# Scores of local attention per 32 queries, turned P through a raster of 512-byte blocks, q and k turned together

## The chip, the cores and the metric

The kernel runs on one NeuronCore of one Trainium2 chip, as one program. The metric is the device time of one execution in microseconds (us). Engine names are those of the profile: PE is TensorE's matmuls and PEld its weight loads, DVE is VectorE, ACT is ScalarE, POOL is GpSimd, SP is SyncE, which here issues nearly all DMAs.

## The reference, cut to what matters

The whole is a recurrent attention layer over 2 sequences of 4096 tokens with 256 channels, followed by two layers of windowed attention with a gated MLP. The change is inside the windowed attention, in each of those two layers:

```python
WINDOW, HEADS, DIM_HEAD = 128, 8, 64
def local_attention(q, k, v):               # q, k are normalised and rotated before
    bq = q.reshape(b, h, w, WINDOW, d) * QK_SCALE
    bk = look_around(k.reshape(b, h, w, WINDOW, d))   # window before + own: 256 keys
    bv = look_around(v.reshape(b, h, w, WINDOW, d))
    sim = einsum('bhwid,bhwjd->bhwij', bq, bk)
    mask = (i < j) | (i > j + WINDOW) | (j == -1)
    attn = softmax(where(mask, -max, sim))
    return einsum('bhwij,bhwjd->bhwid', attn, bv)
```

The mask leaves each query its own key and the 128 before it. A group of 32 neighbouring queries therefore needs at most 160 of the 256 keys of its two windows.

## The kernel before, in words

The program runs stages one after the other (setup, mix, scan, gate, local). The local stage does both layers. It works in units of one window: 128 tokens of one of the two sequences ("streams", `s`), 64 units (`u`, 32 for each layer) per stream, `w` is the unit's parity. The order of work of every engine is written out by hand in a function `half(s, u, w, l)`, of which there are 128. A half runs the attention scores and softmax of unit `u` of stream `s`, and beside them the rest (values, output projection, mean and variance, MLP) of the other stream's unit, called `o, um` in the code; it also projects the next unit of `s`. Engines wait for each other by semaphores alone.

Heads go in four pairs (`hp` 0 to 3). In a half these steps matter here:

- PE: `values(o, 0)`, `values(o, 1)`, `scores(s, 0)`, `scores(s, 1)`, in the second layer `turn_out`, then `values(o, 2)`, `values(o, 3)`, `scores(s, 2)`, `scores(s, 3)`, `project_out`, the three projections (L2473) with `mean` and `variance` between them, `hidden` (L2551, three groups), `out` (L2559). `scores` makes for each head of the pair one matmul, 64 partitions deep, with 128 queries as the stationary operand and 256 keys as the moving one. The two heads of a pair lie on partitions 0 to 63 and 64 to 127 and write two PSUM banks: B and C for even pairs, A of this stream and A of the other for odd ones. `scores(s, 3)` may start when `row_max(s, 1)` has emptied the A banks.
- DVE: `row_max` adds the mask to the scores in PSUM, writes them to `l_prob` in SBUF and takes the maximum in the same pass (L2186), then multiplies the pair's two maxima by a scale (`l_nb`, L2193). Later `inverse_sums` (L2173), the joining of the residual (`attended`, L2219), `deviate` (L2228), and `turn_p` (L2202), which transposes P within blocks of 32 by 32. `turn_q` and `turn_k` do the same for q and k.
- ACT: eight exponentials with row sums (L2367), one for each head, after `head_out` (L2376) has copied the other stream's values out of PSUM.
- POOL: the rotation of k (L2017 to L2022), `normalise` (P times the inverse row sums, L2033), `l_hn` (L2051), which `hidden` waits for, and more.
- SP: the blocks of 32 by 32 are put in their places by a way through DRAM: `write_p` (L1924) stores the turned P of two head pairs, one DMA of 512 KB, and `read_p` (L1932) reads it in four DMAs of 128 KB, one for each 32 partitions. `write_q`/`read_q` and `write_k`/`read_k` do that for q and k. In a half P goes in two groups `g` (pairs 0, 1 and pairs 2, 3); `values(2)` of the next half waits for the second.

The turned keys lie in two slots, `kT[s]`, of which unit `u` writes slot `w`; scores read both, and the mask (`mask[s][w]`, L2186) puts the slots in order. The mask for `w` = 0 is made anew in every second half (`remask`, L2213).

Of the kernel before, what the change touches and what calls it, by code (L numbers as in the profile page):

```python
# [21 lines left out]
ALU = mybir.AluOpType  # L22
# [3 lines left out]
P = 128  # L26
NB = 2
# [1718 lines left out]
def local_stage(nc, persist, a, T):  # L1746
# [7 lines left out]
    BL = P // 32  # L1754
    rows, const, ident = (persist[k] for k in ("rows", "const", "ident"))
    wqkv, wo, w1, w2, b1c, lngb, qks = (persist[k] for k in ("wqkv", "wo", "w1", "w2", "b1c", "lngb", "qks"))
    G = ((0, 1), (2, 3), (4, 5))
    with ExitStack() as ctx:
# [3 lines left out]
        wm = one("wm", [P, 2 * P])  # L1762
        mean_w, pause, least = one("mean_w", [P, P]), one("pause", [P, NB]), one("least", [P, 1])
        x1s, dsqs = two("x1s", [P, P]), two("dsqs", [P, P])
        mask = [two(f"mask{s}_", [P, 2, P]) for s in range(NB)]
# [5 lines left out]
        qT, kT = two("qT", [P, P, NHP]), two("kT", [P, 2, BL, NHP, 32])  # L1771
        V, prob = two("V", [P, 2, HEADS, DH]), two("prob", [P, HEADS, 2 * P])
        pb, pT = two("pb", [P, 2, BL, NHP, 2, 32]), two("pT", [P, 2, BL, NHP, 2, 32])
# [7 lines left out]
        sems = {n: ctx.enter_context(nc.semaphore(f"l_{n}")) for n in ("wm", "set", "prep", "zero", "free", "wqkv", "wo", "w1", "w2", "wiped0", "wiped1")}  # L1781
        R = signals(nc, ctx, "tab", 1, "lr")
        S = signals(nc, ctx, "q_ps k_ps v_ps qsq ksq v_sb ss_q ss_k clamped ln_n rn rq8 kn qm qr k12 kr q_turned k_turned "
                    "q_out:16 k_out:16 qT:64 kT:64 mask0 wo_ps carry x1 x1_sum mean_ps dev dsq dsq_sum var_ps ln_v rstd hn w2_ps hout "
# [61 lines left out]
        def scored(s, hp, x):  # L1846
            return ((bank[s][1], bank[s][2]), (bank[s][0], bank[1 - s][0]))[hp % 2][x][:, 0:2 * P]
# [4 lines left out]
        with nc.Block() as block:  # L1852
            @block.sync
            def _(sp):
# [30 lines left out]
                def write_q(s, u):  # L1885
# [3 lines left out]
                    sp.wait_ge(S["qT"][s].sem, S["qT"][s].after(u, 1))  # L1889
                    sp.sem_inc(sems["free"], 1)  # L1890
                    sp.dma_start(a["qz"][s], q1[s][:].rearrange("p h d -> p (h d)")).then_inc(S["q_out"][s].sem, 16)

                def read_q(s, u):
                    sp.wait_ge(S["q_out"][s].sem, S["q_out"][s].after(u))
                    sp.sem_inc(sems["free"], 1)
                    sp.wait_ge(Q["sc"][s].sem, Q["sc"][s].after(u * NHP - 1))
                    sp.sem_inc(sems["free"], 1)
                    for j in range(BL):
                        sp.dma_start(qT[s][32 * j:32 * j + 32].rearrange("p (i t) h -> p i (t h)", i=BL),
                                     a["qz"][s].rearrange("(i c) (j n) -> j c i n", i=BL, j=BL)[j]).then_inc(S["qT"][s].sem, 16)  # L1900

                def write_k(s, u):
                    sp.wait_ge(S["k_turned"][s].sem, S["k_turned"][s].after(u))
                    sp.sem_inc(sems["free"], 1)
                    sp.wait_ge(S["kT"][s].sem, S["kT"][s].after(u, 1))
                    sp.sem_inc(sems["free"], 1)
                    sp.dma_start(a["kz"][s], k1[s][:].rearrange("p h d -> p (h d)")).then_inc(S["k_out"][s].sem, 16)

                def read_k(s, u, w):
                    sp.wait_ge(S["k_out"][s].sem, S["k_out"][s].after(u))  # L1910
                    sp.sem_inc(sems["free"], 1)
                    sp.wait_ge(Q["sc"][s].sem, Q["sc"][s].after(u * NHP - 1))
                    sp.sem_inc(sems["free"], 1)
                    for j in range(BL):
                        sp.dma_start(kT[s][32 * j:32 * j + 32, w].rearrange("p i h t -> p i (h t)"),
                                     a["kz"][s].rearrange("(i c) (j n) -> j c i n", i=BL, j=BL)[j]).then_inc(S["kT"][s].sem, 16)
# [850 lines left out]
```

## Time and profile before

| what | us |
|---|---|
| median of three runs | 4972.72 (4967.94 to 4975.3) |
| the profiled execution | 4966.22 |
| its span | 4964.4 |
| local stage within it | from about 2257 to the end |

The profile covers one execution. Its span is 1.8 us shorter than that execution's own time, and that time is 6.5 us under the median. Busy time is the time in which an engine had an instruction running; matmuls are pipelined, so that a row's length holds some latency and rows overlap. Starts are us from the span's start. `[0.23 <-issue]` at the end of a row is how long its engine had been idle before it and what ended that.

### The profile page before, as it was taken

The page shows a single profiled execution, that of the slowest core. Times are in us where ns is not written, and L with a number is a line of the kernel's source. Part 1 is how long each engine was busy: PE and PEld are TensorE (multiplying, and loading weights), DVE is VectorE, ACT ScalarE, POOL GpSimd, SP SyncE. Part 2 cuts the span into 40 slices and gives each one's busy share as a digit, 9 for nine tenths or more (in the row PEclk, how much of TensorE's full clock was granted, in tenths as well). Part 3 has the DMA queues.
Part 4 walks back from the last instruction along what each step waited for, and adds up shares of the span by engine and source line. Part 5 has one row for each costly group of instructions (what it writes and reads, how often), then busy time and mean ns, then how long its engine had stood idle before and what let it go on. Part 6 is the DMA issues. An engine that isn't in the chain of part 4 may idle for free. (4 is left out here: it accounts for less than half of the span.)

```text
span 4964.4 us, 269505 instructions
## 1 busy us (share of the span) xinstructions
PE 4507.8 (91%) x107928; PEld 3817.4 (77%) x107928; DVE 3564.7 (72%) x10345; ACT 2979.7 (60%) x8486; POOL 2441.6 (49%) x3196
## 2 busy tenths in 40 slices
PE   7898898678888888666999999999999999999998
PEld 6888888678888888654777777777777777777777
DVE  4666666568878887475777777777777777777775
ACT  5777777534444444354666666666666666666665
POOL 1222222267777777203555555555555555555554
PEclk8999999789999999788999999999999999999999
DMA  2343343467777777694555666555565555555554
GB/s 87 87 96 93 93 98 89 114 143 165 165 165 163 167 164 161 175 299 126 170 170 168 173 174 171 172 171 171 180 196 175 173 173 172 171 171 173 173 175 131
DMA packets 1283528, 775.96 MB, mean 156 GB/s; under 512 B 686800, under 2 KB 1179088, under 8 KB 1282256
## 3 DMA queue, kind: packets, MB, share of 16 engines
q1 hardware_dynamic: 1231888, 700.43, 53.1%
q10 hardware_dynamic: 51392, 73.02, 5.0%
q14 instruction: 190, 1.56, 0.1%
q8 instruction: 58, 0.95, 0.1%
HBM read 410.44 MB, written 362.68 MB: 156 GB/s over the span
## 5 line engine op out<-in xcount | busy, mean ns | idle before, releaser
L2367 ACT ACTIVATE l_prob<-l_prob,l_nb,l_rq 128x256 f32<-128x256 f32 x1024 | 601.6, 590 | 20.8 <-DVE l_nb L2193 13.1
L2033 POOL TENSOR_TENSOR l_prob<-l_prob,l_rinv 128x512 f32<-128x512 f32 x512 | 526.8, 1039 | 108.4 <-DVE l_rinv L2173 108.4
L2017 POOL TENSOR_TENSOR l_k<-l_kn,l_tab 128x512 f32<-128x512 f32 x128 | 162.5, 1270 | 614.8 <-DVE l_kn L2165 614.8
L2559 PE MATMUL lD<-l_hid,w 128*128 128x128 f32 x3072 | 364.0, 275 | 0.0
L2559 PEld LDWEIGHTS lD<-l_hid,w 128*128 128x128 f32 x3072 | 353.3, 192 | 0.0
L2551 PEld LDWEIGHTS lA<-l_hn,w 128*128 128x128 f32 x2048 | 242.9, 195 | 110.1 <-POOL l_hn L2051 61.1
L2202 DVE STREAM_TRANSPOSE l_pb<-l_prob 128x512 f32<-128x512 f32 x512 | 326.6, 676 | 0.6 <-POOL l_prob L2033 0.5
L2027 POOL TENSOR_TENSOR l_qr<-l_q 128x512 f32<-128x512 f32 x128 | 162.4, 1269 | 328.1 <-DVE l_q L2131 328.1
L1097 POOL TENSOR_TENSOR sc_aqx<-sc_late,sc_headmask 128x256 f32<-128x256 f32 x256 | 170.8, 667 | 278.9 <-PE sc_Y L1190 277.2
L1173 PE MATMUL sc_AB<-sc_aq,sc_bkx 32*32 32x32 f32 x16384 | 257.3, 198 | 37.4 <-POOL sc_bkx L1097 29.1
L497 POOL TENSOR_TENSOR rk<-rk,bkraw 128x256 f32<-128x256 f32 x64 | 54.6, 871 | 477.9 <-DVE bkraw L383 477.9
L2551 PE MATMUL lA<-l_hn,w 128*128 128x128 f32 x2048 | 266.0, 284 | 11.8 <-POOL l_hn L2051 5.2
L1115 POOL TENSOR_TENSOR sc_bkT<-sc_tok,sc_headmask 128x128 f32<-128x128 f32 x512 | 263.2, 534 | 0.0
L2524 PE MATMUL lD<-l_oT,wo 128*128 128x128 f32 x2048 | 262.6, 281 | 0.1
L2524 PEld LDWEIGHTS lD<-l_oT,wo 128*128 128x128 f32 x2048 | 238.2, 191 | 29.2 <-issue 28.9
L2473 PE MATMUL lB<-wqkv,l_h 128*128 128x512 f32 x512 | 242.9, 597 | 17.4 <-DVE l_mask L2262 17.2
L2551 PE MATMUL lB<-l_hn,w 128*128 128x128 f32 x2048 | 250.9, 276 | 0.0
L1173 PEld LDWEIGHTS sc_AB<-sc_aq,sc_bkx 32*32 32x32 f32 x16384 | 213.3, 108 | 39.4 <-issue 38.6
L2473 PE MATMUL lC<-wqkv,l_h 128*128 128x512 f32 x512 | 241.0, 593 | 0.0
L2473 PE MATMUL lA<-wqkv,l_h 128*128 128x512 f32 x512 | 240.9, 593 | 0.0
L2551 PEld LDWEIGHTS lB<-l_hn,w 128*128 128x128 f32 x2048 | 240.5, 193 | 0.0
L2193 DVE TENSOR_TENSOR l_nb<-l_mx,l_nrq 128x2 f32<-128x2 f32 x512 | 220.6, 431 | 17.7
(276 smaller groups left out, 13707.3 us busy)
## 6 DMA issues: line engine op xcount, KB each, us to landing
scratch_pz<-l_pb SPq DMA_DIRECT2D x256, 512.0 KB, 3.0
l_pT<-scratch_pz SPq DMA_DIRECT2D x1024, 128.0 KB, 3.2
scratch_cm<-cm SPq DMA_DIRECT2D x64, 512.0 KB, 4.1
scratch_qz<-l_q SPq DMA_DIRECT2D x128, 256.0 KB, 2.9
l_qT<-scratch_qz SPq DMA_DIRECT2D x512, 64.0 KB, 2.0
scratch_kz<-l_k SPq DMA_DIRECT2D x128, 256.0 KB, 2.8
l_kT<-scratch_kz SPq DMA_DIRECT2D x512, 64.0 KB, 2.9
sc_early<-scratch_cm ACTq DMA_DIRECT2D x59, 512.0 KB, 4.7
```

The costliest lines, as they stand in the source:

```text
L1097: return nc.gpsimd.tensor_tensor(dst[:], src.unsqueeze(2).broadcast_to([P, 2 * BG, HQ, CH]), headmask[:].unsqueeze(1).unsqueeze(3).broadca ...
L1115: last = nc.gpsimd.tensor_tensor(bkT[c % 2][:, b * BG:(b + 1) * BG], tok[k][:, c, b, 1:3].rearrange("p x g i -> p (x g) i").unsqueeze(2) . ...
L1173: last = mm(AB_ps[c][at, (x * BG + q) * QH:(x * BG + q + 1) * QH], bkx[c][at, 2 * q + x].rearrange("p h t -> p (h t)"), aq[c][at, q], star ...
L2017: tt(k1[s][:], kn[s][:], wide(2, slice(0, DH)), ALU.mult)
L2033: tt(prob[s][:, pair], prob[s][:, pair], rinv[s][:, pair].unsqueeze(2).broadcast_to([P, 2, 2 * P]), ALU.mult).then_inc(Q["pn"][s].sem, 1)
L2193: tt(nb[s][:, pair], mx[s][:, pair], nrq8[s][:, pair], ALU.mult).then_inc(Q["nb"][s].sem, 1)
L2202: nc.vector.transpose(pb[s][:, g, :, at:at + 2].rearrange("p j h x t -> p (h x) j t"), prob[s][:, 2 * hp:2 * hp + 2].rearrange("p h (x j k ...
L2367: last_ = nc.scalar.activation(prob[s][:, h], prob[s][:, h], ACT.Exp, scale=rq8[s][:, h:h + 1], bias=nb[s][:, h:h + 1], accum_out=sums[s][ ...
L2473: last_ = mm(bank[s][j][:], h[:, k * P:(k + 1) * P], wqkv[:, k, j * INNER:(j + 1) * INNER], start=(k == 0), stop=(k == CC - 1))
L2524: last_ = mm(bank[s][3][:, m * P:(m + 1) * P], wo[:, k, m * P:(m + 1) * P], oT[s][:, k], start=(k == 0), stop=(k == NHP - 1))
L2551: last_ = mm(bank[s][j][0:MW, at:at + P], w1[:, k, tile * MW:(tile + 1) * MW], hn[s][:, k], start=(k == 0), stop=(k == CC - 1))
L2559: last_ = mm(bank[s][3][:, c * P:(c + 1) * P], w2[:, m, c * P:(c + 1) * P], hid[s][:, m], start=(c == 0 and m == 0), stop=(c == CC - 1 and ...
```

## The change

The scores are taken for 32 queries at a time. For each head of a pair there are four matmuls with 32 queries as the stationary operand and 160 keys as the moving one, each writing its own 32 PSUM partitions. Row maximum, exponential, normalising and the transposition of P work on 160 columns for each query instead of 256. The columns of a row are now relative: column `r` of query `32 i + t` is key `32 i + r` of the two windows' 256.

The raster: `write_p` stores each partition's five blocks of 32 keys (512 bytes with four heads) at places in DRAM that lie on diagonals, so that `read_p` finds for each 32 keys the eight blocks of 32 queries, 512 bytes each, of which those never written stay zero. The areas are filled with zeros at the start, four DMAs of 684 KB out of the cleared `pT`.

q and k are turned into one buffer `qk` and go through DRAM with one write and four reads. The turned q and k lie in `qkT` with three slots; a unit with `w` = 1 is written to slot 1, one with `w` = 0 to slot 2, and ACT copies the keys of slot 2 to slot 0 at the end of every half with `w` = 0 (`copy_k`). The mask no longer depends on the parity, and `remask` is gone. In DVE's `half`, `turn_k` and the first two `turn_p` come earlier. PE's waits before `scores` are each followed by a semaphore increment.

```diff
                 def write_p(s, u, g):
...
-                    sp.dma_start(a["pz"][s, g], pb[s][:, g].rearrange("p j h x t -> p (j h x t)")).then_inc(H[g]["p_out"][s].sem, 16)
+                    n = 32 * NHP
+                    sp.dma_start(bass.AP(a["pz"].tensor, (s * 2 + g) * AREA + (BL - 1) * 32 * n,
+                                         [[(2 * BL + 1) * n, P], [32 * n, NR], [1, n]]),
+                                 pb[s][:, g].rearrange("p r h t -> p (r h t)")).then_inc(H[g]["p_out"][s].sem, 16)
                 def read_p(s, u, g):
...
-                        sp.dma_start(pT[s][32 * j:32 * j + 32, g].rearrange("p i h x t -> p i (h x t)"),
-                                     a["pz"][s, g].rearrange("(i c) (j n) -> j c i n", i=BL, j=BL)[j]).then_inc(H[g]["pT"][s].sem, 16)
+                        start = (s * 2 + g) * AREA + (j + BL - 1) * 32 * n
+                        sp.dma_start(pT[s][32 * j:32 * j + 32, g].rearrange("p i x h t -> p (i x) (h t)"),
+                                     bass.AP(a["pz"].tensor, start, [[(2 * BL + 1) * n, 32], [BL * 32 * n, 2 * BL], [1, n]])
+                                     ).then_inc(H[g]["pT"][s].sem, 16)
                 def first():            # SP
...
+                    sp.wait_ge(sems["set"], 1)
+                    for s in range(NB):
+                        for g in range(2):
+                            sp.dma_start(a["pz"][s, g], pT[s][:].rearrange("p g i x h t -> p (g i x h t)")[:, 0:AREA // P]
+                                         ).then_inc(sems["blank"], 16)
                 def first():            # POOL
...
-                        for t in (kT[s], V[s]):
+                        for t in (qkT[s], V[s], pT[s]):
                             nc.gpsimd.memset(t[:], 0.0)
...
-                        nc.gpsimd.memset(mask[s][0][:], MASKED)
+                def copy_k(s, u):       # ACT
+                    act.wait_ge(S["qkT"][s].sem, S["qkT"][s].after(u))
+                    act.wait_ge(Q["sc"][s].sem, Q["sc"][s].after(u * NHP - 1))
+                    nc.scalar.copy(qkT[s][:, 0:BL, 1].rearrange("p i h t -> p i (h t)"),
+                                   qkT[s][:, 2 * BL:, 1].rearrange("p i h t -> p i (h t)")).then_inc(S["kT"][s].sem, 2)
                 def scores(s, u, w, hp):
...
-                    for x in range(2):
-                        rows_ = slice(x * DH, (x + 1) * DH)
-                        last_ = mm(scored(s, hp, x), qT[s][rows_, :, hp], kT[s][rows_, :, :, hp].rearrange("p x i t -> p (x i) t"),
-                                   start=True, stop=True)
+                    own, back = (2, 1)[w] * BL, (1, 0)[w] * BL
+                    for i in range(BL):
+                        for x in range(2):
+                            rows_ = slice(x * DH, (x + 1) * DH)
+                            last_ = mm(scored(s, hp, x)[32 * i:32 * i + 32], qkT[s][rows_, own + i, 0, hp],
+                                       qkT[s][rows_, back + i:back + i + NR, 1, hp], start=True, stop=True)
```

How the order of instructions moves is shown at three places, before and after, from the half with `w` = 0 of a loop body or the first halves. On PE, between the values of the other stream (L2516) and the next values, `lA` to `lD` are PSUM banks; before:

```order
L2516 MATMUL lD<-l_pT,l_V 64x128 x8
L2498 MATMUL lB<-l_kT,l_qT 128x256
L2498 MATMUL lC<-l_kT,l_qT 128x256
L2498 MATMUL lA<-l_kT,l_qT 128x256 x2
L2516 MATMUL lB<-l_pT,l_V 64x128 x8
```

and after:

```order
L2516 MATMUL lD<-l_pT,l_V 64x128 x8
L2498 MATMUL lB<-l_qkT 32x160
L2498 MATMUL lC<-l_qkT 32x160
...
L2498 MATMUL lA<-l_qkT 32x160 x8
L2516 MATMUL lB<-l_pT,l_V 64x128 x8
```

The pair `lB`, `lC` stands four times in a row in the changed kernel, so that two head pairs are 16 matmuls of 160 columns instead of 4 of 256.

On DVE, from the joining of the residual (`l_x_0<-lD,l_h_0`) to the sums of squares (`l_ss<-l_sqk`), `l_pb` being the turned P and `l_dev` what `deviate` makes; before:

```order
L2219 TENSOR_TENSOR l_x_0<-lD,l_h_0 128x2x128
L2173 RECIPROCAL l_rinv<-l_sums 128x2 x2
L2228 TENSOR_TENSOR l_dev<-l_x_0,lD 128x256
L2173 RECIPROCAL l_rinv<-l_sums 128x2
L2202 STREAM_TRANSPOSE l_pb<-l_prob 128x4x4x32 x2
L2158 STREAM_TRANSPOSE l_k<-l_kr 128x4x4x32
L2202 STREAM_TRANSPOSE l_pb<-l_prob 128x4x4x32 x2
L2141 TENSOR_REDUCE l_ss<-l_sqk 128x8
```

and after:

```order
L2206 TENSOR_TENSOR l_x_0<-lD,l_h_0 128x2x128
L2171 RECIPROCAL l_rinv<-l_sums 128x2
L2156 STREAM_TRANSPOSE l_qk<-l_kr 128x4x4x32
L2171 RECIPROCAL l_rinv<-l_sums 128x2
L2198 STREAM_TRANSPOSE l_pb<-l_prob 128x2x5x32
L2215 TENSOR_TENSOR l_dev<-l_x_0,lD 128x256
L2198 STREAM_TRANSPOSE l_pb<-l_prob 128x2x5x32
L2171 RECIPROCAL l_rinv<-l_sums 128x2
L2198 STREAM_TRANSPOSE l_pb<-l_prob 128x2x5x32 x2
L2137 TENSOR_REDUCE l_ss<-l_sqk 128x8
```

The transposition of k and the first of P now stand ahead of `deviate`.

On SP, one half of the first ones; before:

```order
L1899 DMA l_qT<-scratch_qz 32x4x128 x4
L1866 DMA l_rot<-in_rotary 128x256
L1861 DMA l_h_0<-scratch_h 128x2x129
L1924 DMA scratch_pz<-l_pb 128x1024
L1907 DMA scratch_kz<-l_k 128x512
L1924 DMA scratch_pz<-l_pb 128x1024
L1932 DMA l_pT<-scratch_pz 32x4x256 x4
L1915 DMA l_kT<-scratch_kz 32x4x128 x4
L1932 DMA l_pT<-scratch_pz 32x4x256 x4
L1891 DMA scratch_qz<-l_q 128x512
```

and after:

```order
L1868 DMA l_rot<-in_rotary 128x256
L1863 DMA l_h_0<-scratch_h 128x2x129
L1919 DMA scratch_pz<-l_pb 128x5x128
L1898 DMA scratch_qkz<-l_qk 128x1024
L1919 DMA scratch_pz<-l_pb 128x5x128
L1931 DMA l_pT<-scratch_pz 32x8x128 x4
L1909 DMA l_qkT<-scratch_qkz 32x4x256 x4
L1931 DMA l_pT<-scratch_pz 32x8x128 x4
```

The four reads and the write of q are gone as DMAs of their own; q rides with k.

## Rows read from the trace of the kernel before

**Rows 1.** Stretch 2500-4964: PE, PEld, DVE, ACT, POOL busy; granted clock, DMA, GB/s.

```profile
2500.00:4964.00 2464.00, 2432.18 (x17634) 1888.87 (x17632) 1832.00 (x6111) 1605.15 (x4357) 1351.76 (x1532) 1.00 0.59 172
```

**Rows 2.** Line L2524, project_out: ns min/median/max, first and last start.

```profile
L2524 PEld LDWEIGHTS lD<-l_oT,wo x2048: 186/192/192, 2314.4 to 4944.0; 128*128 128x128 f32 x187
```

**Rows 3.** Timeline, PE and PEld, one half of layer 0: start, us, what.

```profile
3026.08 0.60 PE L2498 MATMUL lB<-l_kT,l_qT 64*128 64x256 f32 x1
3026.08 0.60 PE L2498 MATMUL lC<-l_kT,l_qT 64*128 64x256 f32 x1
3026.52 0.39 PE L2498 MATMUL lB<-l_kT,l_qT 64*128 64x256 f32 x1
3026.53 0.39 PE L2498 MATMUL lC<-l_kT,l_qT 64*128 64x256 f32 x1
3026.75 0.64 PE L2498 MATMUL lA<-l_kT,l_qT 64*128 64x256 f32 x4
3027.32 1.09 PE L2516 MATMUL lB<-l_pT,l_V 128*64 128x128 f32 x16
3028.34 0.60 PE L2498 MATMUL lB<-l_kT,l_qT 64*128 64x256 f32 x1
...
3029.18 0.55 PEld L2498 LDWEIGHTS lA<-l_kT,l_qT 64*128 64x128 f32 x4 [0.29 <-DVE l_mx L2186]
3029.95 2.05 PE L2524 MATMUL lD<-l_oT,wo 128*128 128x128 f32 x16
```

**Rows 4.** Timeline, DVE, the same half.

```profile
3026.98 0.42 DVE L2186 CUSTOM_DVE_ANT_0 l_prob<-lB,l_mask 128x256 f32<-128x256 f32 x1 [0.61 <-issue]
...
3027.78 0.64 DVE L2193 TENSOR_TENSOR l_nb<-l_mx,l_nrq 128x2 f32<-128x2 f32 x1
3028.36 0.41 DVE L2186 CUSTOM_DVE_ANT_0 l_prob<-lA,l_mask 128x256 f32<-128x256 f32 x1
...
3029.16 0.16 DVE L2193 TENSOR_TENSOR l_nb<-l_mx,l_nrq 128x2 f32<-128x2 f32 x1
```

**Rows 5.** Timeline, POOL, the same half.

```profile
3026.45 1.27 POOL L2017 TENSOR_TENSOR l_k<-l_kn,l_tab 128x512 f32<-128x512 f32 x1 [4.47 <-DVE l_kn L2165]
```

**Rows 6.** Timeline, end of the projections and start of hidden (L2551).

```profile
3036.83 0.73 POOL L2051 TENSOR_TENSOR l_hn<-l_dev,l_rstd 128x256 f32<-128x256 f32 x1 [0.42 <-issue]
...
3037.83 0.35 PE L2551 MATMUL lA<-l_hn,w 128*128 128x128 f32 x1 [0.16 <-issue]
```

**Rows 7.** Groups by line and form, 2500 to 4964: busy us, mean ns.

```profile
L2367 ACT ACTIVATE l_prob<-l_prob,l_nb,l_rq 128x256 f32<-128x256 f32 x941 | 552.9, 590 | 7.7
L2346 ACT COPY l_V<-lC 128x512 f32<-128x512 f32 x117 | 66.4, 568 | 0.0
L2202 DVE STREAM_TRANSPOSE l_pb<-l_prob 128x512 f32<-128x512 f32 x472 | 301.2, 676 | 0.6 <-POOL l_prob L2033 0.5
L2033 POOL TENSOR_TENSOR l_prob<-l_prob,l_rinv 128x512 f32<-128x512 f32 x472 | 485.7, 1039 | 96.6 <-DVE l_rinv L2173 96.6
```

**Rows 8.** Timeline, SP, the same half.

```profile
3017.28 0.32 SPq L1924 DMA_DIRECT2D scratch_pz<-l_pb  x1
3022.55 1.73 SPq L1932 DMA_DIRECT2D l_pT<-scratch_pz  x4
```

**Rows 9.** DMA issues, 3000 to 3400: packets; KB each, median us to landing.

```profile
DMA packets 69139, 68.17 MB, mean 170 GB/s; under 512 B 7130, under 2 KB 59259, under 8 KB 69115
l_pT<-scratch_pz SPq DMA_DIRECT2D x156, 128.0 KB, 3.2
```

**Rows 10.** Timeline, PE, scan stage at full clock, 32 by 32 tiles.

```profile
1506.22 0.42 PE L1190 MATMUL sc_P<-sc_state,sc_aqx 32*32 32x32 f32 x29 [0.36 <-issue]
```

**Rows 11.** Timeline, start of the local stage.

```profile
2256.95 0.95 POOL L2069 MEMSET l_kT<- 128x1024 f32 x1 [225.59 <-POOLq L104]
...
2262.07 1.40 POOL L2008 TENSOR_TENSOR l_tab<-l_rot,qks 128x256 f32<-128x256 f32 x2
...
2264.14 3.78 PE L2473 MATMUL lB<-wqkv,l_h 128*128 128x512 f32 x4 [17.17 <-DVE l_mask L2262]
```

More of the change, by code:

```diff
@@ L1761, in local_stage @@
         rot, tab = two("rot", [P, 4, DH]), two("tab", [P, 4, DH])
-        wm = one("wm", [P, 2 * P])
+        wm = one("wm", [P, 2, SPAN])
         mean_w, pause, least = one("mean_w", [P, P]), one("pause", [P, NB]), one("least", [P, 1])
         x1s, dsqs = two("x1s", [P, P]), two("dsqs", [P, P])
-        mask = [two(f"mask{s}_", [P, 2, P]) for s in range(NB)]
         hT = [two(f"h{s}_", [P, CC, P + 1]) for s in range(NB)]
@@ L1897, in read_q @@
                     sp.sem_inc(sems["free"], 1)
+                    turned = a["qkz"][s].rearrange("(i c) (j n) -> j c i n", i=BL, j=BL)
+                    cur = (2, 1)[w] * BL
                     for j in range(BL):
[L1899 to L1916, printed above, removed]
+                        sp.dma_start(qkT[s][32 * j:32 * j + 32, cur:cur + BL].rearrange("p i y h t -> p i (y h t)"),
+                                     turned[j]).then_inc(S["qkT"][s].sem, 16)
                 def write_p(s, u, g):
@@ L2260, in first @@
                     for s in range(NB):
-                        nc.vector.tensor_copy(mask[s][0][:, 0, :], wm[:, P:2 * P])
-                        last = nc.vector.tensor_copy(mask[s][1][:].rearrange("p x n -> p (x n)"), wm[:])
-                    last.then_inc(sems["prep"], 1)
-                    dve.wait_ge(sems["prep"], 1)
-                    for s in range(NB):
                         sum_k(s, 0)
@@ L2451, in half @@
                         inverse_norms(s, u + 1)
+                    if w == 0:
+                        copy_k(s, u)
                 def last(s, u, w):
@@ L2587, in half @@
                     if mlp:
-                        values(o, um, 0, layer(um, l))
-                        values(o, um, 1, layer(um, l))
+                        values(o, um, wm_, 0, layer(um, l))
+                        values(o, um, wm_, 1, layer(um, l))
                     scores(s, u, w, 0)
@@ L2594, in half @@
                     if mlp:
-                        values(o, um, 2, layer(um, l))
-                        values(o, um, 3, layer(um, l))
+                        values(o, um, wm_, 2, layer(um, l))
+                        values(o, um, wm_, 3, layer(um, l))
                     scores(s, u, w, 2)
@@ L2707, in lay_out @@
     out["eye16"] = np.ascontiguousarray(np.broadcast_to(np.eye(CH, dtype=np.float32), (P, 2, CH, CH)))
-    q, kx = np.arange(P)[:, None], np.arange(P)[None, :]
-    neg = np.float32(MASKED)
-    before, own = np.where(kx < q, neg, 0), np.where(kx > q, neg, 0)
-    out["winmask"] = np.concatenate([before, own], axis=1).astype(np.float32)
+    row, r = np.arange(P)[:, None], np.arange(160)[None, :]
+    neg, behind = np.float32(MASKED), r - row % 32
+    near = np.where((behind < 0) | (behind > P), neg, 0)
+    begin = np.where(r < P - row // 32 * 32, neg, near)
+    out["winmask"] = np.stack([near, begin], axis=1).astype(np.float32)
     n = out["x"].shape[1]
```

106 lines of the change are left out of this document (53 added, 53 removed).

## The prediction

> **What bounds the kernel now.** I read the page by stages first. From 2500 us to the end, half of the time, PE is busy for 2432 of 2464 us at the full granted clock, while DVE, ACT and POOL are below 75% [rows 1]. Then I read the list of waits: PE hardly waits there, so this stage is PE's own work with a few short holes. The line of `project_out` opens every half: 128 groups of 16, the first at 2314.4, the last 16th at 4944.0, some 1.8 us after its group's first; (4944.0 - 1.8 - 2314.4)/127 gives 20.69 us a half [rows 2]. A microsecond of PE per half is worth 128 us.
>
> The timeline of a half shows what scores cost on PE. Scores of pairs 0 and 1 start at 3026.08 and the next values at 3027.32: 1.24 us. Pairs 2 and 3 start at 3028.34, the next group at 3029.95: 1.61 us [rows 3]. The second is longer because the A banks are free only when `row_max(1)` is through: the weight load at 3029.18 waited 0.29 us for `l_mx`. The reader is to see that this wait is made on DVE: the product `l_nb` of the first pair takes 0.64 us where the next takes 0.16 [rows 4]. It stretches over a POOL operation which runs from 3026.45 to 3027.72, and over the one behind it [rows 5]. I read that as DVE held off its operands by POOL; the small product gets in where one POOL operation ends.
>
> **The scores, PE.** In rows 3, from the second `lB` (3026.52) to the first `lA` (3026.75) is one round: two records of 256 columns side by side, 0.23 us. A pair of heads is two rounds, the group four, 0.92 us; 0.32 us of the 1.24 are start (the first weights) and change to the next shape. A round of 160 columns is 0.23 x 160/256 = 0.144 us. How many rounds there are is the unknown of this change. Now a head pair is eight matmuls on eight different pieces of the array (two halves of the rows, four quarters of the columns), 16 records.
> - All eight abreast: two rounds a pair, four a group, 0.58 us. With 0.27 us of start (smaller weights) 0.85 us.
> - Four abreast: eight rounds, 1.15 + 0.27 = 1.42 us.
> - Two abreast: 16 rounds, 2.30 + 0.27 = 2.57 us.
>
> The trace of before has no eight abreast. Nearest: on the diagonal of 32 by 32 tiles, 29 records take 0.42 us from first start to last end [rows 10], 14 ns each with all latency counted, where one record of 32 columns alone takes 0.23 x 32/256 = 0.029 us. So at least two, with the latency off about three run side by side, on tiles that share neither rows nor columns; and the array takes a new record within 14 ns, while eight abreast ask for one in 18 ns. I take the first, 0.85 us, because both directions of splitting overlap fully where the trace has them singly (heads by rows in rows 3, and the values' 16 records of 128 columns in 1.02 us there, where one by one they would take 1.8), and keep the others for the range.
>
> First group: 1.24 - 0.85 = 0.39 us saved, so the values start at 3026.93 in the clock of rows 3 and pairs 2 and 3 at 3027.95. `row_max(0)` starts at 3026.98 now and could at about 3026.7. A pass over 256 columns takes 0.41 us, one over 160 between 0.26 (all columns) and 0.41 (none); I take 0.31, 0.6 for two. Then `l_nb` waits for POOL's 3027.72, two more passes end at about 3028.3, and `scores(3)` starts at 3028.35 instead of 3029.18 and ends, with half of the group's rounds, at 3028.85. `project_out` comes 1.1 us earlier than 3029.95.
>
> **What is late next.** Nothing between `project_out` and the next scores gets shorter on PE: projections, hidden, out and values are unchanged. There the chain residual, mean, `deviate`, variance, `l_hn` has no room: `l_hn` ends at 3037.56 and hidden starts at 3037.83 after 0.16 us of idle [rows 6]. Three things press on it. The exponentials start later against `project_out`, which comes earlier, though each is shorter: 0.59 us for 256 columns, I take 0.52 (bounds 0.37 and 0.59), 0.5 us for eight. POOL's rotation of k runs 0.9 us further into the half. DVE now has a transposition of k (about 0.67 us) and one of P ahead of `deviate`. DVE waits there for the mean, whose time does not move, so that most of it is hidden; I charge 0.2 us a half (bounds 0 and 0.7, one whole transposition). Sum for a half: -1.1 + 0.2 = -0.9; in layer 1, where `turn_out` and its DVE step lie in the same place, -0.85. Over 64 halves each: -58 - 54 = -112 us.
>
> **Work that is hidden.** A P transposition (676 ns for 512 elements, now 320) and `normalise` (1039 ns likewise) [rows 7] shrink by a third or so: at -0.25 us x 4 on DVE and -0.39 x 4 on POOL. Neither engine is the bound, so I count nothing except that P is turned about 0.7 us earlier. `copy_k` is one ACT copy of 128x512, 0.57 us [rows 7], in every second half, at the half's end, where ACT waits for PE; nothing. If that cover were gone it would cost 64 x 0.57 = 36 us. The copies of the mask and the increments behind PE's waits are small, and PE has a queue of matmuls ahead of them: nothing, bounds -0.2 and +0.2 us a half together.
>
> **The DMAs.** Bytes of P: two writes of 512 KB become 2 x 320 KB, reads stay. Pieces per half: P written 2 x 640 of 512 bytes for 2 x 128 of 4 KB, P read 2048 of 512 bytes for 1024 of 1 KB, q and k written 128 for 256 and read 512 for 1024. Together 3968 for 2560. All engines' packets take on average 0.59 x 16 x 400 us/69139 = 55 ns [rows 1, 9]. 1408 more at that price are 4.8 us on each of 16 engines, share 0.83 at worst; by bytes it falls. I take no change, because the packets get smaller. On the way of P the write is issued at 3017.28, the last reads from 3022.55 to 3024.28, landing 3.2 us after issue, about 3027.1, for values that start at 3027.32 [rows 3, 8, 9]: 0.25 us of room. These must now start at 3026.93. P is turned 0.7 to 1 us earlier and SP issues as many DMAs between write and read as before, so the reads land at about 3026.3. What SP loses (q's write and four reads) stands behind the last read of P and frees nothing here. k arrives before it is needed as now.
>
> **Start.** POOL clears kT and V before; 1024 elements take 0.95 us, 0.9 apart [rows 11]. It now clears 3072 + 1024 + 2048 elements a stream for 2 x 1024, and no mask: +3.3 us a stream, 6.6. PE now starts at 2264.14, waiting for the masks (from 2263.32), behind the `set` of about 2262.1. After: 2268.7. +4.6 us. The zeroing of 2.8 MB in DRAM runs beside the first projections; at the 172 GB/s of rows 1 16 us, before the first P is written some 30 us later: 0.
>
> **Sum.** 4966.2 - 112 + 5 = 4859 for the profiled execution's own time; the median lies 6.5 above it: 4866. The hidden shortening of ACT, DVE and POOL leans down a little; I say 4860.
>
> **Rivals.**
> 1. *Two abreast.* If records ran strictly in the order in which the matmuls are written, a matmul's second record would wait for its first on the same piece and hold up the next matmul: two abreast. Price: +1.33 us in the first group and 2.57 - 1.61 = +0.96 in the second, 2.3 x 128 = 293, with the start and the 6.5 us 5271. From this point on: more than six rounds' equivalent in a group costs time. Against it: the first `lB` and `lC` start within 10 ns, and so do their second ones [rows 3], as if a blocked record did not block the other tile. The Trainium skill, TensorE: Matmul & The Clock Gate, part 3 on packing small matmuls, says that matmuls start and end in program order; by that rule this rival would be the forecast. This is the other side.
> 2. *Four abreast*, because four quarters of columns that read the same rows are not in the trace. First group +0.18, second 1.42 for 1.61, and the freed A banks help no more: 0 a half, with 0.2 for `deviate` at worst: 4978 to 5004, and a little faster where a round takes less than by my scaling; 4978. The Trainium skill's TensorEngine Tiling (Array Packing), theoretical speedup, allows the product of both factors; no run here has shown it.
> 3. *P arrives late.* The write of 640 pieces and the reads of twice as many each land 1 us later (2.9 and 3.2 us now). Reads land at 3028.3 for 3026.93: 1.4 us of wait, of which the hole before `scores(3)` takes 0.6; gain 0.1 to 0.3 us a half, with 0.2 4966 - 26 + 5 + 6.5 = 4952. For it: 640 small writes in DRAM rows 4608 bytes apart have no row here. Against it: idle room on the DMA engines.
> 4. *`deviate` and `l_hn` slip by 0.7 us*: gain 0.4 a half, 4966 - 51 + 5 + 6.5 = 4927; near to my forecast, and counted with it.
>
> **Chances.** Forecast with rival 4: 0.63. Rival 3: 0.12. Rival 2: 0.14, a third each faster, same, slower. Rival 1: 0.08. A mishap not thought of: 0.03, slower. A measurement of this kernel can tell about 0.2%, 10 us, from no change. Faster 0.63 + 0.12 + 0.05 = 0.80; same 0.05; slower 0.15. Range: below, every bound kind (1.35 us a half, no loss at `l_hn`) 4800. Above, to 4965, the near edge of rival 2, which leaves out about 0.18.
>
> **What would show it.** In the profile after: scores groups of about 0.85 us on PE; the load of the A bank's weights about 0.4 us after pair 2's; half length near 19.8 us; the passes over scores near 0.31 us, exponentials near 0.52; hidden starting 0.2 us or more after the last projection; PE's waits for `l_pT` still small; the first projection near 2269. Wrong it is if the groups are 1.4 us or longer (rivals 1, 2), or if the groups are short and the half is still over 20.3 us (rival 3, or a chain I have not priced).

## The result and the profile after

| | before | after |
|---|---|---|
| median, us | 4972.41 (4967.94 to 4975.3, 4 runs) | 4912.78 (4909.06 to 4918.02, 4 runs) |
| ratio | | 0.9882, 95% interval 0.9865 to 0.9899 |
| span of the profiled execution | 4964.4 | 4913.9 |
| half of the last stage, (last - first `project_out`)/127 | 20.69 | 20.22 |
| median of the single halves, layer 0 and layer 1 | 20.41, 20.94 | 20.05, 20.05 |

The change saves 59.6 us where 112 were forecast: the time lies inside the range, 53 us above the value. First the same stretch as [rows 1], of the profile after (window, its length, then busy time and count of each engine, granted clock, share of the DMA engines, GB/s), and the line that opens every half, for [rows 2]:

```profile
2500.00:4914.00 2414.00, 2287.64 (x23383) 1752.74 (x23381) 1588.46 (x6083) 1557.81 (x4433) 1209.18 (x1537) 1.00 0.67 157
```

```profile
L2524 PEld LDWEIGHTS lD<-l_oT,wo x2048: 186/192/333, 2324.2 to 4893.3; 128*128 128x128 f32 x187
```

PE was busy for 98.7% of that stretch and is at 94.8% now; the DMA engines' share rose from 0.59 to 0.67. PE has lost its place as the only bound. Its list of waits in that stretch (line waited in, releaser, us in total, times, longest), of after:

```profile
PE lB L2516 <- DMA l_pT<-scratch_pz: 77.5, 109, 1.4
PE lB L2498 <- DMA l_qkT<-scratch_qkz: 19.2, 18, 1.9
PE lA L2551 <- POOL l_hn L2049: 5.6, 5, 1.7
```

109 of the some 120 halves in it wait for the second half of turned P. The PE timeline at the end of one half shows where, against [rows 3]. Of the 16 `lB` and `lC` records of the first group the first, the eighth, the ninth and the last are shown (the rest is marked by dots):

```profile
3047.26 0.32 PE L2498 MATMUL lB<-l_qkT 64*32 64x160 f32 x1
...
3047.31 0.32 PE L2498 MATMUL lC<-l_qkT 64*32 64x160 f32 x1
3047.42 0.30 PE L2498 MATMUL lB<-l_qkT 64*32 64x160 f32 x1
...
3047.47 0.30 PE L2498 MATMUL lC<-l_qkT 64*32 64x160 f32 x1
3047.56 0.49 PE L2498 MATMUL lA<-l_qkT 64*32 64x160 f32 x16
3049.01 1.09 PE L2516 MATMUL lB<-l_pT,l_V 128*64 128x128 f32 x16 [0.95 <-DMA l_pT<-scratch_pz]
3050.03 0.32 PE L2498 MATMUL lB<-l_qkT 64*32 64x160 f32 x1
```

Eight records start within 0.05 us, the other eight 0.16 us behind: eight abreast, as forecast. The group would hand over to the values after about 0.8 us, but they start 1.75 us behind its start. SP's queue in the same half (start, time to issue, count), from the first write of P on, of after and then of before:

```profile
3035.71 0.40 SPq L1919 DMA_DIRECT2D scratch_pz<-l_pb  x1
3036.44 0.34 SPq L1898 DMA_DIRECT2D scratch_qkz<-l_qk  x1
3037.49 0.36 SPq L1919 DMA_DIRECT2D scratch_pz<-l_pb  x1
3038.52 2.30 SPq L1931 DMA_DIRECT2D l_pT<-scratch_pz  x4
3041.01 1.73 SPq L1909 DMA_DIRECT2D l_qkT<-scratch_qkz  x4
3042.92 1.78 SPq L1931 DMA_DIRECT2D l_pT<-scratch_pz  x4
```

```profile
3035.84 0.34 SPq L1924 DMA_DIRECT2D scratch_pz<-l_pb  x1
3036.44 0.34 SPq L1907 DMA_DIRECT2D scratch_kz<-l_k  x1
3037.62 0.32 SPq L1924 DMA_DIRECT2D scratch_pz<-l_pb  x1
3038.73 1.82 SPq L1932 DMA_DIRECT2D l_pT<-scratch_pz  x4
3040.74 1.73 SPq L1915 DMA_DIRECT2D l_kT<-scratch_kz  x4
3042.64 1.74 SPq L1932 DMA_DIRECT2D l_pT<-scratch_pz  x4
3044.71 0.34 SPq L1891 DMA_DIRECT2D scratch_qz<-l_q  x1
3048.10 1.73 SPq L1899 DMA_DIRECT2D l_qT<-scratch_qz  x4
```

These halves begin (`project_out`) at 3030.66 and 3029.95. The second write of P goes out 6.83 us into the half, for 7.67 before: 0.84 us gained. The second read is issued at 12.26 instead of 12.69: only 0.43 us gained. And each read lands later behind its issue; the list of DMA issues from 3000 to 3400 us has (KB each, median us to landing), where [rows 9] have 3.2 us for `l_pT`:

```profile
l_pT<-scratch_pz SPq DMA_DIRECT2D x159, 128.0 KB, 3.7
l_qkT<-scratch_qkz SPq DMA_DIRECT2D x80, 128.0 KB, 3.8
```

The windows of one half say why. Of after, the 6 us from `project_out`, the 11 us behind them and the rest:

```profile
3030.66:3036.66 6.00, 6.00 (x37) 3.96 (x30) 4.60 (x21) 5.21 (x19) 4.43 (x7) 1.00 0.09 22
3036.66:3047.66 11.00, 10.87 (x112) 9.23 (x119) 6.75 (x17) 7.53 (x18) 2.12 (x4) 1.00 1.09 248
3047.66:3050.66 3.00, 2.05 (x72) 1.37 (x61) 1.67 (x13) 0.61 (x3) 2.92 (x4) 1.00 0.38 96
```

Of before, 7 us, the 9.5 us behind them and the rest:

```profile
3029.95:3036.95 7.00, 7.00 (x33) 4.35 (x32) 5.20 (x20) 5.63 (x18) 5.53 (x8) 1.00 0.22 65
3036.95:3046.45 9.50, 9.34 (x86) 8.52 (x84) 6.66 (x18) 6.07 (x14) 1.87 (x2) 1.00 0.99 273
3046.45:3050.45 4.00, 4.00 (x38) 2.96 (x32) 3.32 (x17) 1.83 (x7) 3.39 (x4) 1.00 0.28 90
```

The share of 0.59 that I had read as room is a mean of 0.99 for 9.5 us and a quarter for the rest. In the kernel before the 16 DMA engines are already full from about 1 us behind the issue of the first write of P until its last read has landed, and they just make it. In the kernel after they are full for 11 us and PE waits for the last read. (The share goes over 1.00 where packets overlap on an engine in the records, so it tells that there was no gap, not how much was moved: that is 273 GB/s in the full stretch of before and 248 in that of after.)

### The profile page after: what moved, and what is told of

Read it like the earlier page. It is cut to its first block and busy times, and to the rows that moved or that the text cites. A ratio compares the mean times of both kernels' runs of the same rounds, so it can differ in the third digit from the quotient of the medians.

```text
span 4913.9 us, 281580 instructions
## 1 busy us (share of the span) xinstructions
PE 4346.3 (88%) x114072; PEld 3665.2 (75%) x114072; DVE 3295.8 (67%) x10277; ACT 2920.9 (59%) x8550; POOL 2290.3 (47%) x3196
## 3 DMA queue, kind: packets, MB, share of 16 engines
q8 instruction: 71, 1.16, 0.1%
## 5 line engine op out<-in xcount | busy, mean ns | idle before, releaser
L2354 ACT ACTIVATE l_prob<-l_prob,l_nb,l_rq 128x160 f32<-128x160 f32 x1024 | 518.4, 509 | 14.3 <-DVE l_nb L2189 14.3
L2031 POOL TENSOR_TENSOR l_prob<-l_prob,l_rinv 128x320 f32<-128x320 f32 x512 | 362.8, 719 | 76.3 <-DVE l_rinv L2171 76.1
L2551 PEld LDWEIGHTS lA<-l_hn,w 128*128 128x128 f32 x2048 | 243.1, 195 | 110.3 <-POOL l_hn L2049 61.1
L2198 DVE STREAM_TRANSPOSE l_pb<-l_prob 128x320 f32<-128x320 f32 x512 | 250.6, 498 | 104.1 <-POOL l_prob L2031 104.1
L2551 PE MATMUL lA<-l_hn,w 128*128 128x128 f32 x2048 | 266.3, 284 | 12.1 <-POOL l_hn L2049 5.6
L2524 PE MATMUL lD<-l_oT,wo 128*128 128x128 f32 x2048 | 264.5, 283 | 0.1
L2524 PEld LDWEIGHTS lD<-l_oT,wo 128*128 128x128 f32 x2048 | 240.1, 193 | 32.7 <-ACT l_oT L2363 30.5
L2551 PE MATMUL lB<-l_hn,w 128*128 128x128 f32 x2048 | 252.0, 277 | 0.0
L2363 ACT COPY l_oT<-lB 128x256 f32<-128x256 f32 x128 | 47.6, 372 | 330.7 <-PE lB L2516 330.7
L2551 PEld LDWEIGHTS lB<-l_hn,w 128*128 128x128 f32 x2048 | 241.7, 194 | 0.0
```

What stands on the lines that cost most here:

```text
L2031: tt(prob[s][:, pair], prob[s][:, pair], rinv[s][:, pair].unsqueeze(2).broadcast_to([P, 2, SPAN]), ALU.mult).then_inc(Q["pn"][s].sem, 1)
L2198: nc.vector.transpose(pb[s][:, g, :, at:at + 2].rearrange("p r h t -> p h r t"), prob[s][:, 2 * hp:2 * hp + 2].rearrange("p h (r k) -> p h ...
L2354: last_ = nc.scalar.activation(prob[s][:, h], prob[s][:, h], ACT.Exp, scale=rq8[s][:, h:h + 1], bias=nb[s][:, h:h + 1], accum_out=sums[s][ ...
L2524: last_ = mm(bank[s][3][:, m * P:(m + 1) * P], wo[:, k, m * P:(m + 1) * P], oT[s][:, k], start=(k == 0), stop=(k == NHP - 1))
L2551: last_ = mm(bank[s][j][0:MW, at:at + P], w1[:, k, tile * MW:(tile + 1) * MW], hn[s][:, k], start=(k == 0), stop=(k == CC - 1))
```

## Experiments

All times are against runs of the kernel before in the same sitting (medians 4965.5 to 4973.7). "Half" is (last - first `project_out`)/127 of the profiled execution, with the median half of layer 0 behind it. "PE's own half" is the length that a half has when PE waits for hardly anything.

| run | median, us | ratio and 95% interval | half, us |
|---|---|---|---|
| after | 4912.8 | 0.9882 (0.9865 to 0.9899) | 20.22, 20.05 |
| pool_order | 4924.7 | 0.9900 (0.9883 to 0.9916) | 20.31, 20.04 |
| p_first | 5279.2 | 1.0615 (1.0598 to 1.0633) | 23.04, 22.71 |
| dve_order | 4990.0 | 1.0029 (1.0019 to 1.0039) | 20.80, 20.60 |
| half_reads | 4817.1 | 0.9687 (0.9671 to 0.9703) | 19.44, 19.19 |
| act_reads | 5055.4 | 1.0169 (1.0152 to 1.0186) | 21.35, 20.72 |
| split_q | 4815.8 | 0.9695 (0.9679 to 0.9712) | 19.51, 19.23 |
| start | 4901.5 | 0.9865 (0.9849 to 0.9882) | 20.20, 20.05 |
| before_order | 4963.0 | 0.9987 (0.9978 to 0.9997) | 20.69, 20.35 |
| best | 4808.6 | 0.9676 (0.9663 to 0.9689) | 19.51, 19.20 |
| best_heads | 4811.4 | 0.9681 (0.9667 to 0.9694) | 19.46, 19.20 |
| scores_twice | 5033.0 | 1.0137 (1.0120 to 1.0154) | 21.22, 20.14 |

**Is P turned too late?** POOL's order alone:

```diff
-                    if mlp:
-                        join_dsq(o, um)
                     normalise(s, u, 3)
+                    if mlp:
+                        join_dsq(o, um)
```

> Changed kernel, but POOL normalises the last pair of heads before it joins the squared deviations. My theory: the half is set by the second read of P, which stands on SP's queue behind four reads of the first half of P and four of q and k (issue from 12.37 us after project_out), long after its write has landed (write issued at 6.83, landing about 3.1). The last transposition of P then ends about 0.45 us earlier (6.2 instead of 6.66), the write goes out earlier, the read does not: median half 20.05 +- 0.05 us, time 4913 +- 10 us, perhaps some us more because variance and l_hn come 0.3 to 0.7 us later. Rival (P is turned too late): the read follows the write, half 19.65, time about 4862.

The second write goes out at 6.43 instead of 6.83 us (median), the second read at 12.4 as before, and the median half is the same, 20.04. PE's list of waits from 2500 to 4800 us says what else happened:

```profile
PE lD L2533 <- POOL l_dsqs L2043: 53.3, 113, 0.5
PE lB L2516 <- DMA l_pT<-scratch_pz: 22.8, 57, 1.4
```

Variance now costs PE 0.47 us a half and the wait for P shrinks by as much: what PE loses elsewhere comes out of that wait, since P comes when it comes. Only layer 1, at 20.37, pays (+12 us in all). And the write that was issued 0.4 us earlier did not land earlier: 10.48 us into the half for 10.51 (medians). Turning the last pair of P earlier is worth nothing.

**SP's order.** `read_p(s, u, 1)` moved ahead of `read_qk`.

> Changed kernel, but SP issues the second read of P before the read of q and k. My theory: the second read is issued from about 10.2 us after project_out and lands near 15.6, so PE no longer waits for l_pT (77 us of such waits before values(2,3) fall to under 10); q and k are read from 12.1 on, land at 17.1 to 17.5 and are needed at 16.5, so that PE waits 0.6 to 1 us a half for l_qkT instead. Half 19.9 to 20.4 us, time 4895 to 4955. Rival (the landing itself, 3.7 us because of 512-byte pieces, or the turning of P, is what comes late): values(2,3) wait as before and the time only rises, 4960 or more with both waits.

The wait for P did vanish from the list, but q and k came far later than I had worked out, with waits of 252 us over 100 halves:

```profile
PE lB L2498 <- DMA l_qkT<-scratch_qkz: 252.2, 100, 4.8
```

q and k are issued from 12.8 us on (12.1 expected), and scores start at 19.1 (17.1 to 17.5 expected). The last of them is issued at 14.2 us; with the usual landing of 3.8 us that gives 18.0. They stand behind 1 MB of P, and that this holds them up is my reading, which no run takes apart. Both theories missed the size (5279), and this made me fold the share of the DMA engines over the half.

A good part of the size is not the wait itself. After such a wait the granted clock falls to its lower level for 3.4 us at a time. The last stage as a whole, and one such stretch, which follows 2.4 us in which PE was idle:

```profile
2500.00:5276.00 2776.00, 2447.66 (x23613) 1860.21 (x23611) 1576.54 (x6141) 1574.51 (x4475) 1218.55 (x1550) 0.94 0.58 138
3103.10:3106.40 3.30, 3.30 (x45) 2.34 (x44) 2.57 (x20) 2.63 (x10) 1.01 (x2) 0.50 0.00 0
```

For the same work PE is busy 20.3 us a half here and 19.2 us in the changed kernel (busy time of the stretch divided by its halves). Over 128 halves that is an estimated 140 of the 366 us by which this run is slower than the changed kernel; the rest is longer waiting.

**VectorE's order undone.** The transpositions of k and P back behind `deviate` and `inverse_sums(3)`.

> Changed kernel, but with VectorE's order of before: all P transpositions and the one of k behind deviate and inverse_sums(3). My theory: the first write of P goes out about 0.7 us later (5.75 instead of 5.05), and with it the first read and all eight DMAs behind it on SP; the second read starts at 13.0 instead of 12.37 and the half grows by 0.5 to 0.7 us, to 20.6 or 20.7: time 4980 to 5000, the whole gain gone. Rival (the order of the transpositions is indifferent since DVE is not the bound and the wait is the landing of the second half alone): 20.05 us, 4913 +- 10.

4990, as my theory had it: the whole gain is gone, with scores, raster and all else as in the changed kernel. The first write of P goes out 0.45 us later (5.50 us into the half for 5.05, medians; I had said 0.7), and the full stretch of the DMA engines starts later with it.

**Half of P's reads.** This kernel reads only the keys of the window before and leaves out P for the query's own window, whose slot stays zero; PE's matmuls are as many as before. Each read has half the pieces and half the bytes. In `read_p` (the slice of `pT` on the line above changes with it):

```diff
-    [BL * 32 * n, 2 * BL], [1, n]])
+    [2 * BL * 32 * n, BL], [1, n]])
```

> Changed kernel, but the reads of P fetch one of the two slots alone, four pieces of 512 bytes a partition instead of eight (the other slot of pT stays zero). It puts a price on the number of pieces. My theory: each of the four DMAs is issued faster (2.3 us for the first four now, towards 1.8) and lands sooner (3.7 us now, 3.1 to 3.3 then), the second half of P lands about 1 us earlier, the wait for l_pT goes, and the half falls to PE's own work, 19.4 to 19.5 us, time 4830 to 4845. Rival A (issue and landing of a DMA have one price whatever it holds): half 20.05, 4913. Rival B (another chain lies just below 20.05, so that the wait moves elsewhere): the wait for l_pT goes and the half stays above 19.8, above 4880.

Landing falls from 3.7 to 2.4 us, that of q and k from 3.8 to 2.9, and the wait is gone. The issue of the first four reads still takes 2.16 us (2.30 in the half shown of after) and of the last four 1.73 (1.78), and the last read is issued no more than 0.14 us earlier: the time on SP hardly changes, the landing does. Whether pieces or bytes make the landing this run can't tell, as both are halved. 19.2 us in layer 0 and 19.5 in layer 1 is PE's own half. One window of 5 us, 12 to 17 us into a half, of half_reads and of after:

```profile
3046.38:3051.38 5.00, 5.00 (x67) 4.55 (x67) 3.03 (x8) 3.51 (x11) 0.01 (x1) 1.00 0.45 129
```

```profile
3042.66:3047.66 5.00, 5.00 (x73) 4.64 (x79) 3.03 (x8) 4.02 (x12) 0.02 (x1) 1.00 1.19 204
```

**SP's issue or the engines' time?** Two of the four reads of the second half of P are issued by ScalarE, in `read_rest`:

```diff
                     if mlp:
                         gelu(o, um, 0, layer(um, l))
+                    read_rest(s, u)
+                    if mlp:
                         gelu(o, um, 1, layer(um, l))
```

> Changed kernel, but two of the four DMAs of the second read of P are issued by ScalarE right behind the first gelu (from about 10.4 us after project_out, where ScalarE waits for PE anyway); SyncE issues the other two, from 12.4. The runs so far leave two theories of why the second half of P is late. Theory A, formed after the first four runs: the 16 DMA engines are busy without a gap from 6.0 to 17.0 us after project_out (share 1.0 in every half microsecond), so the bytes and pieces between the first write and the last read of P set the end, whoever issues them. Then the last piece lands as late as now, the reads that ScalarE puts in delay those of q and k, and the half stays at 20.0 us or grows by up to 0.3: time 4905 to 4955. Theory B: SyncE's issue, 1.8 to 2.3 us for four DMAs, sets it. Then P is complete 0.9 us earlier and the wait of 0.6 us for l_pT goes: half 19.45, time 4835 to 4850.

Theory B is out: an additional queue makes it 143 us slower, not 70 faster. Theory A had the sign and too small a size. The reads issued early land only 5.1 us later, those of q and k grow to 5.0, and PE waits for `l_qkT` 171 us. Some halves cost much more than 0.7 us, and there the clock takes part: in 30 of the 127 halves the mean granted clock is under 0.98, and they last 22.5 us on average, the others 21.0. Why an ordinary half costs 0.7 us more isn't settled.

**q off the full stretch.** q and k in tiles of their own; `write_q` behind the last read of P, `read_q` at the start of the next half:

```diff
+                    if within(un):
+                        read_q(o, un)
...
-                        write_qk(o, un)
+                        write_k(o, un)
...
                     read_p(s, u, 1)
+                    if within(u + 1):
+                        write_q(s, u + 1)
```

> Changed kernel, but q and k go their separate ways again, as before the change: q is written behind the last read of P (14.8 us after project_out) and read at the start of the next half, when the DMA engines are idle; only k is written and read between P's write and read. Scores, raster and the copy of k stay. Theory A (the DMA engines' time between 6 and 17 us): q's write of 256 KB (0.7 us of all 16 engines) and its read of 512 pieces (1.2 to 1.3 us) leave that stretch, the second half of P lands 1.5 us or more earlier, no wait for l_pT is left and the half is PE's own, 19.2 to 19.4 us: time 4815 to 4840. Theory B (SyncE's issue): as many DMAs are issued between the write and the second read of P as in the changed kernel, so nothing is gained: 4905 to 4920.

4815.8. The same number of DMAs stands between P's write and second read as in the changed kernel, and all of P's raster is as it was; only q's 256 KB each way have left that stretch. The wait for P is gone, so 512-byte pieces of P alone don't make P late. The windows of one half (6 to 12 us, 12 to 17 us) show the hole that this makes, where after has 1.02 and 1.19:

```profile
3031.65:3037.65 6.00, 5.88 (x41) 4.60 (x41) 3.72 (x9) 3.51 (x8) 2.12 (x3) 1.00 0.97 261
3037.65:3042.65 5.00, 5.00 (x68) 4.55 (x68) 3.03 (x8) 3.50 (x11) 0.02 (x1) 1.00 0.68 185
```

And SP's four first reads of P take 1.83 us to issue again, not 2.30. So both ways in which the load delayed P show here: the last read of P is issued 0.5 us earlier than in the changed kernel and lands 1.9 us earlier (13.2 and 16.3 us into the half for 13.7 and 18.2, medians). half_reads, where the issue hardly moved, says that the landing is the larger part.

**The start.** POOL makes `mean_w` and the tables first and clears behind them.

> Changed kernel, but POOL makes the mean weights and the rotation tables first and clears qkT, V and pT behind them, and only the blanking of the raster and the copy of V wait for the clearing. PE's first projection then starts about 10.5 us earlier (where the mean weights are set at 2272.5 now, about 2262), the rest of the chain follows: time 9 to 11 us less, 4902 to 4904. If the clearing on POOL, which now runs beside the first rotations, or the blanking, which runs beside the writes of q and k, holds up something that is as late, the gain is 0 to 5 us: 4908 to 4913. In either case the half stays at 20.05.

11 us less (8 by the two ratios). In after, the clearing is on the path from the stage's start to the first projection:

```profile
2261.21 2.66 POOL L2067 MEMSET l_qkT<- 128x3072 f32 x1 [226.94 <-POOLq L104]
2272.81 3.53 PE L2462 MATMUL lB<-wqkv,l_h 128*128 128x512 f32 x4 [21.53 <-POOL l_mean_w L2072]
```

**VectorE's order alone,** in the kernel before.

> The kernel before with the one part of the change that is VectorE's order (k and the first pair of P are turned ahead of deviate). In the kernel before PE does not wait for P, so an earlier P gives nothing; the transposition of k (0.67 us) and the one of P (0.68 us) stand before deviate, which runs 4.03 us after project_out and may be late by up to 0.7. Theory: 4973 +- 10 if deviate is hidden, up to 5010 if it slips. Rival (the order itself brought the gain of the change): 4915 to 4940.

4963, 0.13% faster: nothing that matters. `deviate` is hidden. The order pays only where PE waits for P.

**Both gains together.**

> Both gains so far together: q and k apart (half 19.2 in layer 0, 19.5 in layer 1, measured 4815.8) and POOL's clearing behind the first projections (11.4 us measured alone). They lie in different stretches of the program, so they should add up: 4815.8 - 11.4 = 4804 +- 5 us. If not, the clearing on POOL now collides with the first write of q that has come back ahead of it: 4808 to 4816.

4808.6, which lies within both expectations, so that they aren't told apart: 104 us faster than the changed kernel, 161 than the kernel before.

**Do eight small matmuls need the heads by turns?** Only the two loops over the matmuls swapped.

> The kernel of the run above, but the eight matmuls of a pair of heads are written head by head (four quarters of the columns on the same rows, then the other four), where the two heads took turns. Theory: the eight small matmuls lie on eight different pieces of the array and run abreast in either order, as the profile after shows for the first order (eight first records within 0.05 us, the eight second 0.16 us behind them): first eight records within 0.05 to 0.06 us again, time the same within 5 us, 4804. Rival (quarters that read the same rows share a way in, and only the alternation of the heads hides it): the four of one head start one round, 0.16 us, apart from the others or from each other, each group of scores grows by 0.16 to 0.6 us and the time by 40 us or more, 4845 to 4960.

The same time, the intervals overlap. Its profile:

```profile
3003.13 0.34 PE L2523 MATMUL lB<-l_kT,l_qT 64*32 64x160 f32 x4
3003.15 0.34 PE L2523 MATMUL lC<-l_kT,l_qT 64*32 64x160 f32 x4
3003.29 0.32 PE L2523 MATMUL lB<-l_kT,l_qT 64*32 64x160 f32 x4
3003.31 0.32 PE L2523 MATMUL lC<-l_kT,l_qT 64*32 64x160 f32 x4
```

The four of one head start within 0.02 us of the four of the other, on the same rows or not.

**The price of the scores.**

> The combined kernel (4808.6, PE hardly waits in it), but each of the eight matmuls of scores of a pair of heads is issued twice (the second pass writes the same values again). It takes the price of the scores on PE by itself. Theory (eight abreast): the extra eight matmuls are two more rounds a pair, 0.144 to 0.16 us each, four a group, two groups a half: +1.15 to +1.3 us a half over 128 halves: 4955 to 4975. Rival (the records lie abreast in the profile only because their starts are put there and the array serves four at a time): four more rounds a pair, +2.3 to 2.6 us a half, 5100 to 5140. If the scores were hidden behind something else as late: under +0.6 us a half, below 4885.

5033 is between the theories, and the median half tells them apart: 20.14 against 19.20, +0.94 us. The first group grows from 0.72 to 1.25 us (expected 0.58 to 0.64 more), the second from 1.00 to 1.25, because it had waited for a bank (medians of layer 0). 0.16 us of the 0.94 are not in the two groups, and I have no account of them. Four abreast would have asked for 2.3 to 2.6, so eight abreast it is. The rest, some 110 us, is in 27 long halves, nearly all of them every fourth one. In these PE stands still, and then the granted clock is at its lower level for some us; the line of the first matmuls and the window behind the idle stretch:

```profile
3262.00 1.97 PE L2541 MATMUL lD<-l_pT,l_V 128*64 128x128 f32 x16 [4.11 <-issue]
```

```profile
3262.00:3266.00 4.00, 4.00 (x80) 3.12 (x80) 0.62 (x6) 0.37 (x1) 1.17 (x1) 0.50 0.24 69
```

The same 16 matmuls take 1.09 us at full clock. The list of waits has 79.0 us of standing still in 22 halves, 3.6 us each; the clock makes most of the rest. The profile's list of DMA queues has, for scores_twice, this line (packets, MB), where best and after have 71 packets and 1.16 MB:

```profile
q8 instruction: 327, 5.36, 0.4%
```

A pass of PE's loop is four halves, with one branch. In the trace it has grown from some 1660 instructions (matmuls, weight loads and what the sequencer runs) to some 2170. The 256 packets more are 16 KB each, 8 for each of 32 passes: the instructions are now fetched anew in each pass. The Trainium skill, Runtime: NRT & Kernel Launch, Instruction fetch mechanics, gives PE room for 2048 instructions and says that a taken branch to a target outside the pages held must wait until the target's page is fetched. The two kernels lie on either side of that number, and the trace agrees.

## Why the prediction was right in direction and half off in size

- **Scores on PE:** right. Eight abreast. Where PE doesn't wait for P (best), the two groups take 0.72 and 1.00 us, 1.13 less than the 2.85 of before, forecast 1.1. By half_reads and split_q PE's own half is 19.2 us in layer 0 and 19.5 in layer 1, 1.2 and 1.4 under before. The Trainium skill's TensorEngine Tiling, theoretical speedup, allowed the product of both splits, and the trace agrees. The Trainium skill's rule of program order (TensorE: Matmul & The Clock Gate, part 3), by which rival 1 would have been the forecast, does not hold as I applied it: in the trace a matmul's second record starts 0.16 us behind its first and doesn't hold up the next matmul's first, which starts 6 to 10 ns behind its forerunner.
- **`row_max`, exponentials, P transposition, `normalise`:** 0.32, 0.51, 0.50 and 0.72 us, forecast 0.31, 0.52, about 0.43 and 0.65. Hidden, as said.
- **`deviate` and `l_hn`, 0.2 us a half:** it cost nothing. `l_hn` ends 7.58 us after `project_out` and hidden starts at 7.64, for 7.60 and 7.66 before (medians of layer 0).
- **`copy_k`, the increments on PE:** nothing, as forecast. The copy takes 0.60 us, 15.9 us into the half.
- **Start:** +4.6 forecast. From the stage's first clearing to the first `project_out` it is 63.0 us for 57.5: +5.5. The profiled execution entered the stage 4.3 us later as well, in code that is the same; that is no part of the change.
- **DMAs: the step that failed.** It was: P is turned 0.7 to 1 us earlier, SP issues as many DMAs between write and read as before, "so the reads land at about 3026.3", with no change of load "because the packets get smaller". The count was right and the wrong thing to count. The change had put q's write and read, 256 KB each, into the same DMAs as k's, that is from behind the last read of P to ahead of it, into the stretch where the 16 engines have no room. I had noted that they had stood "behind the last read of P" and so free nothing, not where they went. Counted from `project_out` (medians of layer 0), the first read of P is issued 0.97 us earlier than before, as forecast; but SP takes longer over it, so that the last read is issued only 0.33 us earlier, and that one lands 4.5 us behind its issue instead of 3.3. It lands at 18.24 us for 17.36: 0.88 us later, where some 0.8 us earlier was forecast. Two things of size follow: the stretch is 11 us of full share instead of 9.5, and packets of 512 bytes of P are no bargain. By the share of the DMA queue from 3000 to 3400 us the DMA engines' time a half went from 0.592 x 20.4 = 12.1 us to 0.663 x 20.07 = 13.3, with 11% fewer bytes a half. In the half shown P is complete at 18.35 us, where PE is ready for it at 17.40.
- **Rivals:** the outcome is rival 3's, P late, at another price. I had it at 4952 with 0.12, because I asked only whether each transfer lands later by itself. PE's gain of 1.2 to 1.4 us a half became a wait of about 0.7 and a gain of 0.36 in layer 0 and 0.89 in layer 1. Both layers now have the same half, 20.05, though PE's own work differs between them: the bound is off PE. That the time still lies well inside the range is in part luck, since its upper end was drawn for rival 2 and the missing 53 us came from the way that I had given 0.12.
- **My own test** was "groups short and the half over 20.3". At 20.05 it did not fire; the wait for `l_pT`, of which I had said that it stays small, was the sign that failed.

## What to carry to other kernels

Before a change makes an engine faster, fold the share of the DMA engines over one period: a mean of 0.59 was 0.99 over the half that mattered. When two transfers are merged, ask of each where in the order its bytes stood; what leaves an idle stretch for a full one delays all that stands behind it (here the last read of P lands 1.9 us later than with q kept out). If a median period is the same in two parts of a program in which one engine has different work, look for the bound outside that engine. And where an experiment makes TensorE stand still in every period, read the granted clock before pricing the wait: in p_first the clock made an estimated 140 of 366 us.

## What the runs showed of the hardware

- Eight matmuls of 64 rows by 32 columns run abreast: 16 records of 160 columns for a pair of heads in two rounds of 0.13 to 0.16 us, in either order of writing.
- The time to issue four reads on SP hardly follows their size (1.73 us for four of 64 KB in half_reads, 1.78 for four of 128 KB in after). It was longer right behind large writes: 2.30 us behind a write of 512 KB and one of 320 KB, and 1.83 with q's 256 KB out of the first.
- A second issuing queue didn't help while the engines were full: ScalarE's reads landed after 5.1 us, and those of q and k went from 3.8 to 5.0.
- A loop body of some 2170 instructions on PE cost about 5 us in nearly every pass, 3.6 of them standing still; one of some 1660 cost nothing that shows.
- The granted clock fell to its lower level (0.50) in or behind idle stretches of PE of 2.4 us (p_first) and 4.1 us (scores_twice). There `project_out` takes 2.75 us for 2.05, and 16 values matmuls 1.97 for 1.09.
